# First attention: a second set of scores, by keys, in place of the transposes of the probabilities

## The reference

```python
B, S, D, H = 16, 112, 256, 16          # batches, queries, width, heads; HD = D // H = 16; 375 keys
x1 = layernorm(x)
xq, xk, xv = x1 @ wq, ctx @ wk, ctx @ wv       # split into 16 heads of 16
scores = einsum('bhqd,bhkd->bhqk', xq, xk) / sqrt(HD) + mask    # mask: [1, 1, 112, 375]
attn = softmax(scores, axis=-1)
x = x + einsum('bhqk,bhkd->bhqd', attn, xv).reshape(...) @ wo
```

## Time and profile before

| what | us |
|---|---|
| median of 3 runs | 1063.67 (1060.84 to 1070.55) |
| profiled execution, first to last instruction (its span) | 1064.7 |
| first attention, first head's scores to last head's exponential | 33.6 to 384.5 |
| first experts' first products begin | about 411 |

### The profile page before, as it was taken

The page is one execution under the profiler, slowest core; times in us unless marked ns, Lnnn a source line. Parts: engine busy times, 40 slices in busy tenths (PEclk is TensorE's granted clock), DMA queues, the critical chain, the costliest instruction groups (busy, mean ns, idle before and its releaser), DMA issues.

```text
span 1064.7 us, 22763 instructions
## 1 busy us (share of the span) xinstructions
PE 936.9 (88%) x7879; PEld 852.9 (80%) x7879; DVE 688.3 (65%) x1947; ACT 545.8 (51%) x1208; POOL 461.6 (43%) x438
## 2 busy tenths in 40 slices
PE   5889998898899865999999939972999999999997
PEld 4778787787788755899999926652999999999987
DVE  6556674575567565777777627875667877787443
ACT  3768886786788655565556514331333333333220
POOL 2022234322521324766667642555355455445514
PEclk9899998898899886999999969985999999999999
DMA  7878887776756416677877576644354254335101
GB/s 188 166 205 190 199 202 190 207 183 168 201 136 141 109 50 190 176 205 181 221 188 207 149 165 176 211 140 148 145 141 113 85 140 114 93 110 137 21 5 22
DMA packets 110035, 160.21 MB, mean 150 GB/s; under 512 B 11600, under 2 KB 98992, under 8 KB 107984
## 3 DMA queue, kind: packets, MB, share of 16 engines
q1 hardware_dynamic: 95968, 140.16, 48.9%
q0 software_dynamic: 13936, 18.33, 8.6%
HBM read 103.45 MB, written 56.96 MB: 151 GB/s over the span
## 4 chain that ended last, share of the span: by engine, by line
PE 50%; DVE 6%; DMA 3%; issue 2%; POOL 1%; ACT 1%; another core or an unknown queue 0%; POOLq 0%; SPq 0%; DVEq 0%
PE ps L326 41%; PE ps L605 2%; PE ps L622 2%; PE ps L517 2%; DVE HTH L1349 1%; DMA x_scratch<-XG 1%; PE ps L673 1%; DMA XG<-xg_scratch 1%; PE ps L345 1%; PE ps L340 1%; DMA X<-x_scratch 1%; PE ps L613 0%; DVE o_end L967 0%; POOL x_scratch L1617 0%; PE ps L690 0%
## 5 line engine op out<-in xcount | busy, mean ns | idle before, releaser
L326 PE MATMUL ps<-XGH,WH 128*128 128x280 f32 (+1 forms) x768 | 220.3, 287 | 2.8 <-DVE GT L1345 2.2
L326 PE MATMUL ps<-XGL,WH 128*128 128x280 f32 (+1 forms) x768 | 221.6, 289 | 0.0
L326 PE MATMUL ps<-XGH,WL 128*128 128x280 f32 (+1 forms) x768 | 221.2, 288 | 0.0
L1221 DVE CUSTOM_DVE_ANT_0 NS<-ps,negm 112x375 f32<-112x375 f32 x256 | 137.9, 545 | 111.5 <-PE ps L432 104.9
L1605 POOL TENSOR_TENSOR HTL<-GT,HTH 128x280 fp32r<-128x280 f32 x112 | 115.1, 1030 | 159.8 <-DVE HTH L1349 159.8
L778 ACT ACTIVATE PP<-NS,MN 112x375 f32<-112x375 f32 x256 | 156.1, 610 | 3.4 <-DVE MN L1221 2.8
L440 PE MATMUL ps<-cst,PP 112*125 112x112 f32 x768 | 141.2, 295 | 17.8 <-ACT PP L778 14.6
L326 PE MATMUL ps<-WH,HTH 128*128 128x256 f32 (+1 forms) x536 | 152.9, 285 | 2.5 <-POOL HTL L1605 2.4
L326 PEld LDWEIGHTS ps<-XGH,WH 128*128 128x128 f32 x768 | 147.9, 193 | 3.8 <-DVE GT L1345 2.8
L326 PE MATMUL ps<-WL,HTH 128*128 128x256 f32 (+1 forms) x536 | 150.4, 281 | 0.0
L326 PE MATMUL ps<-WH,HTL 128*128 128x256 f32 (+1 forms) x536 | 150.1, 280 | 0.0
(11 more groups left out here) (211 smaller groups left out, 1898.3 us busy)
## 6 DMA issues: line engine op xcount, KB each, us to landing
WG<-in_v SPq DMA_DIRECT2D x48, 512.0 KB
KST<-k_scratch SPq DMA_DIRECT2D x48, 376.0 KB, 5.5
WG<-in_w SPq DMA_DIRECT2D x32, 512.0 KB
k_scratch<-KHL SPq DMA_DIRECT2D x64, 188.0 KB
CT<-in_ctx_t SPq DMA_DIRECT2D x32, 375.0 KB, 6.7
xg_scratch<-zero SPq DMA_DIRECT2D x8, 1289.8 KB
xg_scratch<-zero SPq DMA_DIRECT2D x16, 586.2 KB, 9.7
XG<-xg_scratch SPq DMA_DIRECT2D x14, 536.0 KB, 3.8
```

The source lines that it names most:

```text
L326: m = e.matmul(out_ap, l, r, start=n == 0, stop=n == len(steps) - 1)
L1221: e.tensor_tensor_reduce(out=NS[:, n % 4, :], in0=ps[0:S, n % 3, 0:KEYS], in1=negm[:], scale=1.0, scalar=3.0e38, op0=ALU.add, op1=ALU.min, ...
```

## The change

The scores are computed twice. The first set, by rows, is as before, but only its minimum is used: `NS` is still written and read by nobody. Every eight heads, PE transposes the eight minima (`minima_turned`), ACT and DVE split them into a high and a low part (`minima_hi`, `minima_lo`), and SP copies these as two rows, 96 and 97, under the stacked queries (`minima_rows`); the keys get two rows of -1 there. The second set (`probs`) has keys as rows: for four heads and 125 of the keys, two matmuls of 98 contraction rows and 224 columns (two heads each) give minus the score plus the maximum, already turned. DVE adds the turned, negated mask `MKT` between PSUM and SBUF (`probs_masked`, 125 x 448), ACT takes the exponential in place (`probs_exp`, 125 x 448), and the values are multiplied from there. The three transposes a head, their copy and the exponential by rows are gone. The new steps come LAG = 17 steps behind the first scores, `heads_values` 24 steps behind; the output of a batch comes one batch later, and the loop has 16 steps more. `KST` has three buffers in place of two, and SP's order is another.

```diff
-NPT = 8
+ROWS_KQM = 98
+NKST = 3
+LAG = 17
+GQ = 4 * S
+        def probs_due(n):
+            k, c = divmod(n - LAG, 4)
+            return (k, c) if 0 <= k < N // 4 and c < 3 else None
+        def minima_due(n, h):
+            i, at = divmod(n - h, 8)
+            return i if at == 0 and 0 <= i < N // 8 else None
-            return [divmod(n, H) for n in range(N + 3 * H)]
+            return [divmod(n, H) for n in range(N + 4 * H)]
...
-            def head_transposes(n):
-                e.wait_ge(exp_done, n + 1)
-                if n >= 2:
-                    e.wait_ge(cp_done, n - 1)
-                for c in range(3):
-                    t = e.transpose(ps[0:KC, 3 + n % 2, c * S:(c + 1) * S], PP[:, n % 4, c * KC:(c + 1) * KC], ident[0:S, 0:S])
-                t.then_inc(pt_done, 1)
+            def minima_turned(i):
+                bk = pe_bank(e, ("mn", i), ml_done, i + 1)
+                e.wait_ge(min_done, 8 * (i + 1))
+                e.transpose(ps[0:8, bk, 0:S], MN[:, i % 2, :], ident[0:S, 0:S]).then_inc(full(bk), 1)
+            def probs(k, c):
+                b, j0 = k // 4, 2 * (k % 4)
+                n = 3 * k + c
+                if k == 0 and c == 0:
+                    e.wait_ge(setup, 9)
+                if k % 2 == 0 and c == 0:
+                    e.wait_ge(d_mrow[k // 2 % 2], 32 * (k // 4 + 1))
+                if n >= 2:
+                    e.wait_ge(masked, n + 1)
+                bk, o = 3 + n % 2, b % 2 * S
+                keys = slice(c * KC, (c + 1) * KC)
+                logits = ps[0:KC, bk, 0:GQ].rearrange("p (h s) -> p h s", h=4)
+                for i in range(2):
+                    m = e.matmul(logits[:, 2 * i:2 * i + 2, :], KST[0:ROWS_KQM, b % NKST, j0 + i, keys],
+                                 QST[0:ROWS_KQM, b // 2 % 2, (j0 + i) // 4, :, (j0 + i) % 4, o:o + S], start=i == 0, stop=i == 1, skip_group_check=True)
+                m.then_inc(pr_done, 1)
...
             for b, h in batch_order():
                 n = b * H + h
-                if 0 <= n - 3 < N:
-                    head_transposes(n - 3)
                 if n < N:
                     head_scores(n)
-                if n % 4 == 0 and 0 <= n - 8 < N:
-                    heads_values(n - 8)
+                if probs_due(n):
+                    probs(*probs_due(n))
+                if n % 4 == 0 and 0 <= n - LAG - 7 < N:
+                    heads_values((n - LAG - 7) // 4)
+                if minima_due(n, 9) is not None:
+                    minima_turned(minima_due(n, 9))
...
-            def head_exp(n):
-            def head_copy(n):
+            def minima_hi(i):
+                bk = ready(e, ("mn", i))
+                if i >= 2:
+                    e.wait_ge(d_mrow[i % 2], 32 * (i // 2))
+                e.activation(MH[:, i % 2, :], ps[0:8, bk, 0:S], ACT.Copy).then_inc(mh_done, 1)
+            def probs_exp(k, c):
+                n = 3 * k + c
+                e.wait_ge(masked, n + 3)
+                e.activation(PT[:, k % 2, c, :], PT[:, k % 2, c, :], ACT.Exp, scale=-1.0).then_inc(exp_done, 1)
...
+            def probs_masked(k, c):
+                n = 3 * k + c
+                e.wait_ge(pr_done, n + 1)
+                if n == 0:
+                    e.wait_ge(masked, 2)
+                if k >= 2:
+                    e.wait_ge(pv_done, k - 1)
+                e.tensor_tensor(PT[:, k % 2, c, :].rearrange("p (h s) -> p h s", h=4), ps[0:KC, 3 + n % 2, 0:GQ].rearrange("p (h s) -> p h s", h=4),
+                                MKT[:, c:c + 1, :].broadcast_to([KC, 4, S]), ALU.add).then_inc(masked, 1)
...
                 if 0 <= n - 1 < N:
                     head_min(n - 1)
+                if probs_due(n - 1):
+                    probs_masked(*probs_due(n - 1))
+                if minima_due(n, 10) is not None:
+                    minima_lo(minima_due(n, 10))
...
+            def minima_rows(i):
+                b, hf = divmod(i, 2)
+                e.wait_ge(ml_done, i + 1)
+                for t, half in enumerate((MH, ML)):
+                    p = ROWS_KQ + t
+                    e.dma_start(QST[p:p + 1, b // 2 % 2, hf, :, :, b % 2 * S:(b % 2 + 1) * S].bitcast(F32).rearrange("p u j s -> p (u j) s"),
+                                half[:, i % 2, :].bitcast(F32)).then_inc(d_mrow[i % 2], 16)
...
-            for b in range(B):
+            for b in range(B + 1):
+                if b % 2 and 3 <= b < B - 1:
+                    stack_q((b + 1) // 2)
+                if 1 <= b < B - 1:
+                    write_k(b + 1)
                 if b and b % 2 == 0 and b + 2 < B:
                     write_q(b // 2 + 1)
-                    stack_q(b // 2 + 1)
+                if b:
+                    minima_rows(2 * b - 1)
+                if 1 <= b < B - 1:
+                    stack_k(b + 1)
+                if b < B:
+                    minima_rows(2 * b)
                 if b + 4 < B:
                     context(b + 4)
-                if b + 2 < B:
-                    write_k(b + 2)
-                    stack_k(b + 2)
```

More of the change, by code:

```diff
@@ L45 @@
 ROWS_KQ = 96
-NPT = 8
+ROWS_KQM = 98
+NKST = 3
+LAG = 17
+GQ = 4 * S
+QA = 64
 NY = 4
@@ L69, in use, with build_kernel @@
         return bank, before
-def build_kernel(nc, x, ctx_n, ctx_t, mask, bmask, wq, wk, wv, wo, wrt, w1, b1, w2, b2, gw, v1, v2, v3, const, out):
+def build_kernel(nc, x, ctx_n, ctx_t, mask, mask_t, bmask, wq, wk, wv, wo, wrt, w1, b1, w2, b2, gw, v1, v2, v3, const, out):
     top = ExitStack()
@@ L113, in build_kernel @@
         ident = cst[:, C_ID:C_ID + 128]
+        O = ExitStack()
+        MH = sb("MH", [8, 2, S], F32R, at=O)
+        ML = sb("ML", [8, 2, S], F32R, at=O)
+        O.close()
         ov = {n: sb("o_" + n, [128, *shape], dt) for n, shape, dt in (
@@ L305, in counts_due @@
         def counts_due(step, n=0):
-            late = {3: H * B + 7, 4: H * (B + 1) + 8}
-            at = {c: late.get(c, H * (b0 + nb + 1) + 11) for c, (b0, nb) in enumerate(CHUNKS0)}
+            late = {3: H * (B + 1) + 7, 4: H * (B + 2) + 8}
+            at = {c: late.get(c, H * (b0 + nb + 2) + 11) for c, (b0, nb) in enumerate(CHUNKS0)}
             return next((c for c in at if at[c] + n == H * step[0] + step[1]), None)
@@ L485, in pe_attention0 @@
                         project_q(b // 2 + 2)
-                if 1 <= b <= B:
+                if 2 <= b <= B + 1:
                     if h == 8:
-                        project_out(b - 1)
+                        project_out(b - 2)
                     if h == 13:
-                        route_x(b - 1)
+                        route_x(b - 2)
                 if after_logits((b, h), 0) is not None:
@@ L819, in act_attention0 @@
                     x_hi(b + 3 + h - 10)
-                if 1 <= b <= B and h == 14:
-                    x2_out(b - 1)
+                if 2 <= b <= B + 1 and h == 14:
+                    x2_out(b - 2)
                 if after_logits((b, h), 1) is not None:
@@ L1217, in head_min, with minima_lo @@
                 if n == 0:
-                    e.wait_ge(negm_done, 1)
-                if n >= 4:
-                    e.wait_ge(exp_done, n - 3)
-                e.tensor_tensor_reduce(out=NS[:, n % 4, :], in0=ps[0:S, n % 3, 0:KEYS], in1=negm[:], scale=1.0, scalar=3.0e38,
-                                       op0=ALU.add, op1=ALU.min, accum_out=MN[:, n % 4:n % 4 + 1]).then_inc(min_done, 1)
+                    e.wait_ge(masked, 1)
+                if n >= 2:
+                    e.wait_ge(min_done, n - 1)
+                at = n % 2 * 4 + n // 2 % 4
+                e.tensor_tensor_reduce(out=NS[:, n % 2, :], in0=ps[0:S, n % 3, 0:KEYS], in1=negm[:], scale=1.0, scalar=3.0e38,
+                                       op0=ALU.add, op1=ALU.min, accum_out=MN[:, n // 8 % 2, at:at + 1]).then_inc(min_done, 1)
+            def minima_lo(i):
+                bk = 6 + banks.at["mn", i][0]
+                e.wait_ge(mh_done, i + 1)
+                if i >= 2:
+                    e.wait_ge(d_mrow[i % 2], 32 * (i // 2))
+                e.tensor_tensor(ML[:, i % 2, :], ps[0:8, bk, 0:S], MH[:, i % 2, :], ALU.subtract).then_inc(ml_done, 1)
+            def probs_masked(k, c):
[7 more added lines that the diff above has]
+                                MKT[:, c:c + 1, :].broadcast_to([KC, 4, S]), ALU.add).then_inc(masked, 1)
             def values_turned(b):
@@ L1563, in context_lo @@
                 e.tensor_tensor(CL[:], CT[:, b % 2, :, :], CH[:], ALU.subtract).then_inc(cl_done, 1)
-            e.memset(VV[:, :, :, :, HD:2 * HD], 1.0).then_inc(setup, 1)
+            e.memset(VV[:, :, :, :, HD:HD + 1], 1.0).then_inc(setup, 1)
             e.memset(zero[:], 0.0).then_inc(setup, 1)
@@ L1827, in sp_attention0 @@
                         sp_chunk(e, n)
-                if b and b % 4 == 0:
-                    kept(b - 4)
+                if b >= 6 and b % 4 == 2:
+                    kept(b - 6)
             kept(B - 4)
```

139 lines of the change are left out of this document (71 added, 68 removed).

## The result

| kernel | median us | runs | ratio to before, 95% |
|---|---|---|---|
| before | 1063.6 | 1060.84 to 1070.55 | |
| changed | 1085.91 | 1083.30 to 1088.77 | 1.0203 [1.0164, 1.0242] |

The change costs 22 us, 2.0%, where 13 were forecast. The span is 1085.0 us. The loop of the first attention, from the first scores at 33.3 us to the last exponential at 401.8, takes 368.5 us for 350.9 before. (The trace of the kernel before has the first scores at 33.2 us, not at 33.6 as the table ahead of the prediction says; the loops then stand 368.5 to 351.3.) In the profiled executions the end of the loop comes 17.3 us later, the first experts' first product 18.4 us later (427.8 for 409.4), and the span is 20.3 us longer; the medians differ by 22.3.

A forecast was written before the change was run, and what follows sets the result against it. DVE was to become the bound in place of the PE-ACT ring: 318 + 20 + 15 + 3 + 5 = 361 us against 350.9, plus 2 at the end and 1 at the start, 13 slower: 1077 us (own range 1066 to 1090).

The forecast's parts named there:

- DVE's work in the loop: First attention: 212 us busy plus 104 of mask additions and 6 of minima splits, taken as 318 us (312 to 328).
- waits in the new ring: PE may write a chunk only once DVE has added the one two chunks earlier: 20 us, from nothing to 58.
- lower clock: First attention: PE below full clock for 49 us, DVE starving 31% of it: 15 us, bounds 0 and 40.
- the loop's end: Batch 14's `route_x` stands ahead of the last chunks in PE's order and waits for POOL: 3 us.
- SP at b = 6: Weights (2 MB) and zeros stand ahead of the next batch's writes: one late landing, 5 us, bounds 0 and 37.
- start: Before the loop, the turned mask is loaded ahead of rows of x and negated: 1 us, 0.3 to 2.
- the 60 that the prediction named as its failure: First attention: the forecast is wrong if DVE has more than 60 us idle.
- about 40: Expected sign in the first attention: DVE idle about 40 us before minima and additions, with PE as releaser.
- rival three: Each first half's minima rows land 2 us late in all 16 batches: 32 us instead of 5; 1104, chance 0.10.
- the 1113 us: Total if each of 448 large DVE instructions cost 0.08 us more by the pipeline-drain rule, 36 us in all.
- rival two: First attention: clock falls more often, 130 us lower instead of 49, DVE starving 40 instead of 15; 1102, chance 0.15.
- One: First attention: PE keeps DVE fed and the lower clock hardly comes, loop 330 us; 1046, chance 0.25.

The follow-up runs named there:

- three_banks: Changed kernel with three PSUM banks for the chunks of second scores and two for the first scores, instead of two and three: 1091.20 us, ratio to before 1.0281.

## Why the prediction was right, and where its terms were off

The direction and the main reason held: the mechanism was the forecast's own, DVE becomes the bound, and the time lay in the forecast's own range (1066 to 1090). Its size was 9 us short. By the steps:

| term | forecast | measured |
|---|---|---|
| DVE's work in the loop | 318 | 312 |
| waits in the new ring | 20 | 15, all of DVE's idle time in the windows at full clock |
| lower clock | 15 | 22, in the windows below it, from 64 us on |
| the loop's end, SP at b = 6 | 3 + 5 | in the two above: 6.9 behind the last minimum, 0.6 at b = 6 |
| DVE idle in the first 30 us | 0 | 19, of which 12.6 the late rows |
| loop | 361 | 368.5 |
| routing behind the loop | 2 | 1.1, to the experts' first product |
| start | 1 | 0: first scores at 33.3 for 33.2 |

That the time fell into the own range is in part luck: the work, the ring and SP at b = 6 were taken 6, 5 and 4 us too high, and they cover a good part of the 19 us at the start for which the sum had nothing. DVE was idle 56.6 us, nearer to the 60 that the prediction named as its failure than to its "about 40". A wait of PE at `probs` for the minima, the sign of rival three, was there too, but once and at the start.

- **DVE's work** was the right thing to add up, and the spacing was the right price. The timeline of DVE after:

```profile
76.38 0.62 DVE L1279 TENSOR_TENSOR PT<-ps,MKT 125x448 f32<-125x448 f32 x1
76.92 0.54 DVE L1253 TENSOR_TENSOR KHL<-ps,KHL 128x376 fp32r<-128x376 f32 x1
77.38 0.54 DVE L1262 CUSTOM_DVE_ANT_0 NS<-ps,negm 112x375 f32<-112x375 f32 x1
...
77.84 0.62 DVE L1279 TENSOR_TENSOR PT<-ps,MKT 125x448 f32<-125x448 f32 x1
```

An addition costs 0.54 us from start to start, as worked out from the neighbour of equal size, and the operations around it 0.46. The term came out 6 us high. The prediction weighed the rule of the Trainium skill, VectorE: DVE Perf Modes, section The DRAIN you can't avoid, that the next operation waits for an empty pipeline, and found the spacing to contradict it. It left out how the section goes on: "A next op that is not held starts earlier". With that sentence the trace agrees: here each of these operations, which don't need each other's result, starts about 0.08 us before the recorded end of the one before it. So the 1113 us was the price of half a rule.

- **The start** is the step that was missing. The forecast priced it by what had to be loaded more (the turned mask, 1 us) and asked for late rows at b = 6, because 2 MB of weights stand there. It did not walk SP's queue through the first batch, where 1.1 MB of x, the tables and eight weight loads stand ahead of rows that hadn't existed before. PE has only two waits for `ML` in the whole loop, 14.1 us, and the first of them is 13.5. The other is the late landing expected behind the 2 MB of weights; it cost 0.6 us, not 5. The runs with other orders gave back 2.4 to 10.5 us, not 12.6, because the wait partly moved to later rows. All of it was not removed in any run, so what a start without late rows would give was not measured.
- **The end** was taken at 7 us of additions and 3 us of waits. Behind the last minimum lie 17 us, of which DVE works 10.1 and is idle 6.9. Every run has such a tail, 16 to 23 us from the last minimum to the last exponential. None made the distance of 17 steps shorter, so what a shorter tail would give back was not measured.
- **The lower clock** came more often, 88 us over the whole loop where 49 were taken. From 63 us on to the last 30 us it was about as forecast (39 for 34 before); the rest lies at the start, where PE stood still for the late rows, and at the end, where the first scores run out. The share of it in which DVE starves was about right from 64 us on (22.4 / 67 = 33% for 31%, with the ring's waits in those windows counted in); the amount of such time was not. Part of this idle time may belong to the stall that goes ahead of the lower clock rather than be its price. This was not separated. TensorE: Matmul & The Clock Gate, section A second HAM failure mode: psum-queue depth-cycling, of the Trainium skill, reports of another kernel that short idle times between groups of matmuls make the clock swing. Here the stretch from 124 to 176 us held a clock of 1.00 with PE idle 9.5 of 52 us, so the rule holds in direction at most, and rival two's 130 us did not come.
- **The ring** cost less than its 20 us, and three_banks, which gave it a bank at the expense of the first scores' ring, gained nothing.
- **The rivals.** One (DVE kept fed, 1046) describes the loop from 124 to 176 us, where DVE was 96% busy, but neither the start nor the end. Two and three did not happen at their sizes, and three not at its place. Two came nearest: 88 us at the lower level instead of 130, and its 40 us of DVE's idle time are there in the windows of the whole loop below the full clock (41 us), but 12.6 of them are the late rows. ACT's exponential took 577 ns instead of 0.68 us, which changes nothing, for ACT waits 121 us.

In sum the change took 270 us of work from ACT (and gave 111 back) and some 20 from PE (319 us busy before, 297 now), and put 99 us on the engine that became the bound by it.

## What to carry to other kernels

Before work is moved from one engine to another, add up the receiving engine's whole loop by start-to-start spacings; once that sum is the largest, further time on it counts about fully (here 56 us gave 53.5), and an operation that can be had from an engine below its limit, here a mask as one more matmul, is worth trying first. Where a change adds a small transfer that the first iteration needs, walk through the issuing queue from the start of the program and not only in the steady loop. Where it puts work many steps behind, count the steps that run alone at the end. When one late transfer is moved up, look for the next in the same queue: two orders in a row moved the wait to a later row, and a third left it there.

## What the runs showed of the hardware

- A matmul of 448 columns in fp32r took 0.22 us from start to start at full clock. With 192 of them added the granted clock of the loop was 0.96 for 0.91, and the loop 10 us longer. Adding 384 of 224 columns, 42 us, to a loop bound by DVE cost 12 us.
- The issue of the same eight loads by SP took 3.7 us ahead of 1120 KB of x on the queue and 7.6 us behind them. The two rows of minima issued at 67.7 us and at 65.3 us ended PE's wait at the same time, 72.5 and 72.6 us.
- A two-operand addition of 125 x 448 from PSUM took 616 ns and the next began 0.54 us after its start. The exponential of the same tile took 577 ns from SBUF (L824) and 540 from PSUM:

```profile
L830 ACT ACTIVATE PT<-ps 125x448 f32<-125x448 f32 x192 | 101.2, 540 | 17.5 <-PE ps L483 16.0 <-issue 0.3
```
